# Cross attention of two layers: another order of TensorE's steps within each iteration

## What is computed

```python
h = concatenate([x, latents], axis=1)                  # 512 keys: context and latents
q = (latents @ q_w + q_b).reshape(b, k_len, 16, 16)    # 16 heads of 16
kv = (h @ kv_w + kv_b).reshape(b, p + k_len, 16, 16, 2)
attn = einsum('bkhd,bnhd->bhkn', q, kmat) / 16
attn = where(full_mask, attn, -inf)
attn = softmax(attn, axis=-1)
attn_out = einsum('bhkn,bnhd->bkhd', attn, v)
attn_out = attn_out @ out_w + out_b + residual
```

## Time and profile before

| what | value |
|---|---|
| median of 3 runs | 1532.18 us (1531.98 to 1532.39) |
| the profiled execution | 1532.83 us |
| its span, first to last instruction | 1531.0 us |
| mean granted TensorE clock | 0.933 |
| PE busy, share of span | 1348.4 us, 88% |
| DVE busy | 1068.1 us, 70% |
| ACT busy | 690.1 us, 45% |
| POOL busy | 430.8 us, 28% |
| ACT exponentials of the attention (L1337), layers 1 to 3 | 192, 194.9 us, 1026 ns each |
| DVE maxima (L1361), layers 1 and 3 | 256, 173.2 us, 690 ns each |
| PE scores (L1432) | 256, 127.6 us, 510 ns each |

### The profile page before, as it was taken

The page is one execution under the profiler, slowest core; times in us unless marked ns, Lnnn a source line. Parts: engine busy times, 40 slices in busy tenths (PEclk is TensorE's granted clock), DMA queues, the critical chain, the costliest instruction groups (busy, mean ns, idle before and its releaser), DMA issues. The chain is left out here.

```text
span 1531.0 us, 28408 instructions
## 1 busy us (share of the span) xinstructions
PE 1348.4 (88%) x8938; PEld 1078.1 (70%) x8938; DVE 1068.1 (70%) x2588; ACT 690.1 (45%) x1406; POOL 430.8 (28%) x480
## 2 busy tenths in 40 slices
PE   2799999995699999996997999697999986799959
PEld 2699999984699999985864655584666663466548
DVE  6488888877488888887655885655666656588575
ACT  1366666663266666664411655312444421056531
POOL 2644444431744444431130000302111103000020
PEclk7899999998799999998997999796999997799989
DMA  4000000102100000100135341203000003633120
GB/s 137 28 29 29 28 27 27 34 0 73 35 29 29 28 27 27 34 0 28 59 115 115 82 88 32 70 1 110 23 21 23 24 18 122 138 80 79 35 68 28
DMA packets 74462, 75.92 MB, mean 50 GB/s; under 512 B 9216, under 2 KB 61174, under 8 KB 73866
## 3 DMA queue, kind: packets, MB, share of 16 engines
q1 hardware_dynamic: 73512, 74.76, 17.9%
q10 hardware_dynamic: 866, 0.09, 0.0%
HBM read 58.19 MB, written 16.26 MB: 49 GB/s over the span
## 5 line engine op out<-in xcount | busy, mean ns | idle before, releaser
L1337 ACT ACTIVATE s_probT<-s_st_ps 128x1024 f32<-128x1024 f32 x192 | 194.9, 1026 | 212.3 <-PE s_st_ps L1453 131.8
L1361 DVE TENSOR_REDUCE s_mx<-s_s_ps 128x1 f32<-128x512 f32 x256 | 173.2, 690 | 48.5 <-PE s_s_ps L1432 43.1
L651 ACT ACTIVATE a_prob<-a_s_ps,a_negmax 128x257 f32<-128x257 f32 x256 | 119.2, 477 | 101.9 <-DVE a_negmax L732 101.9
L1432 PE MATMUL s_s_ps<-l_k_st,l_q_st 127*128 127x512 f32 x256 | 127.6, 510 | 16.6 <-PEq L1120 13.3
L592 POOL TENSOR_TENSOR a_v_hi<-a_v_sum,x_one 128x512 fp32r<-128x512 f32 x64 | 67.4, 1054 | 251.1 <-DVE a_v_sum L721 251.1
L1317 POOL COPY l_v_st<-l_v_all 128x16 f32 (+3 forms) x64 | 18.9, 300 | 397.0 <-PE s_o_ps L1464 337.1
L1464 PE MATMUL s_o_ps<-s_probT,l_v_st 128*32 128x256 f32 x1536 | 120.0, 390 | 2.1 <-ACT s_probT L1337 1.9
L732 DVE TENSOR_REDUCE a_negmax<-a_s_ps 128x2 f32<-128x514 f32 x128 | 86.8, 688 | 44.1 <-PE a_s_ps L794 43.1
L747 DVE TENSOR_TENSOR a_pT_lo<-a_t_ps,a_pT_hi 128x512 fp32r<-128x512 f32 x128 | 88.3, 690 | 38.2 <-ACT a_pT_hi L664 36.4
L664 ACT ACTIVATE a_pT_hi<-a_t_ps 128x512 fp32r<-128x512 f32 x128 | 76.8, 600 | 66.3 <-PE a_t_ps L848 63.3
L1432 PEld LDWEIGHTS s_s_ps<-l_k_st,l_q_st 127*128 127x128 f32 x256 | 52.2, 205 | 77.3 <-DVE s_mx L1361 40.0
(11 more groups left out here) (206 smaller groups left out, 4045.7 us busy)
## 6 DMA issues: line engine op xcount, KB each, us to landing
l_k_st<-k_stack SPq DMA_DIRECT2D x96, 128.0 KB
l_q_st<-q_stack SPq DMA_DIRECT2D x96, 64.0 KB, 2.2
x_wqk_raw<-L_xattn_wq SPq DMA_DIRECT2D x32, 128.0 KB, 2.3
x_wqk_raw<-L_xattn_wk SPq DMA_DIRECT2D x32, 128.0 KB, 2.3
x_wv_raw<-L_xattn_wv SPq DMA_DIRECT2D x16, 256.0 KB, 3.2
a_wo_raw<-L_xattn_wo SPq DMA_DIRECT2D x16, 256.0 KB, 3.1
k_stack<-p_k_hi SPq DMA_DIRECT2D x4, 1024.0 KB, 5.2
k_stack<-p_k_lo SPq DMA_DIRECT2D x4, 1024.0 KB, 6.1
```

The lines of the kernel that those rows point to most:

```text
L651: nc.scalar.activation(prob[:, n % 2, qt, 0:NK], s_ps[:, n % 2, qt, 0:NK], ACT.Exp, bias=negmax[:, n % 2, qt:qt + 1], accum_out=den[:, n % ...
L1337: nc.scalar.activation(probT[:, (s + 2) % U, n], st_ps[:, 2 * (n % 2):2 * (n % 2) + 2].rearrange("p k t -> p (k t)"), ACT.Exp).then_inc(z. ...
L1361: nc.vector.tensor_reduce(mx[:, s, n:n + 1], s_ps[:, n % 2, 0:c.NK], AX.X, ALU.max).then_inc(z.max_done, 1)
L1432: mm = nc.tensor.matmul(s_ps[:, n % 2], q_st[0:m, s, j, qt * P:(qt + 1) * P], k_st[0:m, s, j], start=True, stop=True)
```

## The change

One line of the tables is replaced. The scores are issued two by two, P0 comes ahead of E0, P2 and P3 stand together, and E2 comes behind them. The number of steps of each kind is the same, and no other engine's table is touched.

```diff
     else:
-        pe_steps = steps("S0 E0 S1 M0 P0 S2 P1 S3 E1 S4 P2 S5 E2 S6 P3 S7 E3 X0")
+        pe_steps = steps("S0 S1 P0 E0 M0 S2 S3 P1 E1 S4 S5 P2 P3 E2 S6 S7 E3 X0")
         act_steps, dve_steps = steps("E0 E1 E2 O0 E3"), steps("S0 S1 S2 M0 S3 S4 S5 S6 S7 X0")
```

## The result

The changed kernel takes 1551.51 us (median of 4 runs, 1547.95 to 1554.85) against 1532.29 for the kernel before. The ratio is 1.0125, 95% interval 1.0102 to 1.0148: slower by 19 us. The forecast was 1558.4 with a range of 1547 to 1567. The direction and ScalarE's (ACT's) part of the mechanism hold; VectorE's (DVE's) part was taken too large, and the loss is 19 us, not 26.

A forecast was written before the change was run, and what follows sets the result against it. PE bounds the kernel at 7.235 us an iteration; a ring of waits makes it 8.03. Per layer 13 x 0.80 = 10.4 us plus 2.7 for the last iterations, 26.2 us for both: 1558.4 us, range 1547 to 1567.

The forecast's parts named there:

- PE sets the pace: Attention's steady part before the change: PE busy 79.36 of 79.59 us, 7.235 us an iteration, nothing keeping it waiting.
- The saving of 0.36: P2 and P3 adjacent on PE save 0.36 us an iteration, bringing PE's own work from 7.18 to 6.82.
- X0 waits for O0: Late in each iteration, PE's X0 waits 0.51 us for ACT's O0, which stands behind exponential 2.
- P0 for exponential 3: PE's P0 waits 0.28 us for ACT's fourth exponential, free 2.99 us behind E2.
- The ring: Closed chain of waits from P0 through PE, DVE's maxima and ACT back to P0, 7.98 us an iteration.
- M0 to S2: Distance on PE from M0's start to S2's, taken as 0.13 us, as from X to S.
- S5 waits 0.33: PE's S5 waits 0.33 us for DVE's maximum of S3, at 2.27 behind S2 instead of 1.94.
- the maximum of S3 0.38 later: On DVE, the maximum of S3 starts 0.38 us after DVE's M0 and lasts 0.69.
- S3 and S7 do not: PE's S3 and S7 do not wait: two maxima start 0.60 apart, PE needs over 1.6 from pair to pair.
- the first rival: Only the ring through ACT binds and DVE's part hides: 7.65 us an iteration, 1550 us; chance 12%.
- Iterations 16 and 17: Stage's end: E0 behind P0 makes P0 come every 6.73 and 6.64 us instead of 5.33, together 2.7 us.
- The clock: Rival: TensorE's clock falls to 1.2 GHz because PE idles more, costing more than 160 us; chance 2%.

The follow-up runs named there:

- The last experiment: Only PE's table changed against the kernel before: P in two pairs, E2 early, S never paired where VectorE is late; 1519.45 us, ratio 0.9919.
- O0 early: The changed kernel with ACT's copy O0 moved ahead of exponential 2; 1542.81 us, ratio 1.0068.
- M early: Against spread with O0 early, M0 moved forward on PE (four steps) and on DVE (behind S2 again); 1517.58 us, ratio 0.9904.
- M early with O0 late: Against M early, only ACT's O0 put back behind exponential 2; 1530.91 us, ratio 0.9990.
- Tail alone: Against the changed kernel, PE's head put back to the order before, the changed tail (P2, P3 ahead of E2) kept; 1550.58 us, ratio 1.0121.
- E2 back: The changed kernel with E2 moved ahead of P2 and P3 on PE; 1541.35 us, ratio 1.0070.
- E0 first with E2 back: The changed kernel with E2 ahead of P2 and P3 and E0 ahead of P0, four pairs of S kept; 1535.6 us, ratio 1.0031.
- spread with O0 early: Against the changed kernel: P in two early pairs, X0 ahead of S7, DVE's M0 behind S4, ACT's O0 ahead of exponential 2; 1547.54 us, ratio 1.0099.

## Why the prediction was right, and where its sums were off

**PE sets the pace, and the place to look is what now waits.** Right. PE's new open waits are 5.1 us in eleven iterations, in which the time grew by 5.5 us (79.59 to 85.12).

**The saving of 0.36 for P2 and P3 side by side.** The 1.00 for two is measured (862.27 to 863.27). The last experiment, 13 us faster with two such pairs and no ACT wait, fits a saving, but it moves other steps too. The 0.36 was not measured alone.

**X0 waits for O0, P0 for exponential 3.** Right in place and close in size. From E2's load to P0 are 3.09 us (863.27 to 866.36); the prediction's 2.99 counts from a point 0.11 later, since it books the open weight load before E2, and the trace books it inside (E2 lasts 0.74 instead of 0.64). So this leg is met within 0.01. That O0's place costs was shown twice: by O0 early (7 to 9 us less than the change) and by M early against M early with O0 late (13 us, one line apart).

**The ring, leg by leg.** Foretold 7.98, measured 858.63 to 866.36, 7.73. The prediction had P0 to S2 1.29, measured 1.18. It had S2 to P2 2.27 + 0.32 = 2.59, measured 2.46 (859.81 to 862.27). P2 to E2 was 1.11 and is 1.00 to the load, 1.11 with it. The last leg is met. So two legs hold the whole error of 0.25: P0 to S2 with 0.11 and S2 to P2 with 0.13. Here is where they come from:

- M0 to S2 was taken as 0.13, as from X to S, and is 0.03 (859.78 to 859.81).
- **The term that failed** is "S5 waits 0.33", and in it "the maximum of S3 0.38 later" than DVE's M0. DVE in the timeline of the changed kernel:

```profile
858.76 1.28 DVE L1361 TENSOR_REDUCE s_mx<-s_s_ps 128x1 f32<-128x512 f32 x2
860.32 0.69 DVE L1361 TENSOR_REDUCE s_mx<-s_s_ps 128x1 f32<-128x512 f32 x1 [0.29 <-PE s_s_ps L1432]
860.93 0.27 DVE L1400 TENSOR_SCALAR s_mxT<-s_x_ps 8x128 fp32r<-8x128 f32 x1
861.12 0.67 DVE L1361 TENSOR_REDUCE s_mx<-s_s_ps 128x1 f32<-128x512 f32 x1
```

It is 0.19 (860.93 to 861.12). In the kernel before, the 0.38 of the earlier trace rows was no price of DVE: S3 started at 882.07 and lasted 0.50, so the maximum at 882.60 had waited for its data. A distance that ends with an arrival was read as a duration. The change issues S3 directly behind S2, and its data are there early. The maximum of S3 is now done at 861.79, and the pair S4, S5 lasts 0.67 instead of 0.63, so S5 waits about 0.04 us and not 0.33. Tail alone shows the other case: there S3 ends at 877.71, the maximum of S3 starts 0.39 behind M0, and S5 does wait 0.33.

- In exchange a wait came that the prediction had excluded, "S3 and S7 do not". The maximum of S1 ends at 860.04, since DVE does its X between the maxima 7 and 0 and X0 is late, and S3 stands in a pair of 0.78 instead of 0.63, 0.15 us late. The statement had counted only the rate of the maxima, not where they start.

The measured ring is thus only 0.08 above the one through ACT alone, the first rival (7.65, 1550 us, 12%), and the time of 1551.5 lies by that rival and not by the forecast of 1558.4. That it lies in the range is owed to the range reaching down past this rival. The ring through ACT sets the iteration of the change, and the waits on maxima add 0.2 where 0.33 was foretold. Behind it lies a second limit that the prediction did not add up: with ACT's waits gone, three versions with all four pairs of S (O0 early, E2 back, and E0 first with E2 back) stop at 7.46 to 7.47 and not at PE's 6.82. No version takes the pairs of S apart and keeps P2 and P3 ahead of E2, so what the pairs cost while ACT's waits are there is not shown.

**Iterations 16 and 17.** Foretold 6.73 and 6.64, measured 6.62 and 6.54. In iteration 16 the 0.11 lies half before E2 and half behind it: with 0.11 for E2's load, P0 to E2 is 3.69 (943.83 to 947.41), foretold 3.74, and from there to P0 2.93, foretold 2.99. E0 behind P0 is a part of the cause and not the whole: for the last two iterations E2 back gives 12.1 us against the 13.2 of the change, and E0 first, added to it, 10.6.

**Sum.** 13 x 0.50 + 2.5 = 9.0 for each layer, 18.1 in both, against the 26.2 foretold. The whole difference is 0.80 against 0.50 in an iteration. Of it 0.25 is the ring of the iteration shown. The rest is small things: most other iterations of the change take 7.68 to 7.75 from X0 to X0, many a little less than the 7.73 shown, and the one in which the loop jumps back (iteration 8) is 0.4 over the others where before it was 0.5 over them.

**The clock.** It stays at 1.00 with PE busy for 94% of the steady part (80.04 of 85.12), so that rival had nothing to stand on.

## What to carry to other kernels

In a software-pipelined loop with a fixed order on each engine, write down for each step who releases it and how far behind its release it stands. Grouping steps to save PE time can shorten exactly these distances, and an engine whose table is left alone may then serve in the wrong order: here O0 behind exponential 2 cost 13 us in one pair of versions. Before a distance from a trace is put into a sum, check whether the later instruction had its data already; if it hadn't, the distance is the supplier's. And when steps are moved, the slow hand-overs count too: a copy by DMA that had 5.7 us until its reader put 1.95 us on the path once the steps stood close.

## What was not expected of the hardware

A matmul with full weights after the transpose with 8 columns of weights (M0) starts only 0.03 us after it (859.78 to 859.81), 0.10 less than after X's two transposes in the earlier trace rows. A reduction starts 0.19 us behind the start of DVE's M0 when its data are there (860.93 to 861.12), although M0 is listed with 0.27. The copy of eight rows of maxima into one row of `q_st` takes 1.95 us from DVE's end to PE's start in the version spread with O0 early, of which 0.66 is the issue.
